# A gated feed-forward and an FP4 feed-forward as one stage, with the FP4 weights quantised between the gated products

## The reference

```
# end of block 5 (XN holds the block's input plus its gated attention, "y")
y2 = y * rsqrt(mean(y*y) + 1e-6) * ff_norm_w
y  = y + (silu(y2 @ ff_w1) * (y2 @ ff_w3)) @ ff_w2        # 256 -> 1024 -> 256
x  = x + y
# block 6, on layernorm(x): a feed-forward whose inputs and weights go through FP4
def fp4_quant_dequant(x):              # blocks of 16 along the last dimension
    scale = max(max|x| / 6, 1e-12);  q = nearest of 0 .5 1 1.5 2 3 4 6, with sign
    return q * scale
gate, up = fq(x) @ fq(w_gate).T, fq(x) @ fq(w_up).T       # 256 -> 704
x = x + fq(silu(gate) * up) @ fq(w_down).T                # 704 -> 256
```

## Time and profile before

| | us |
|---|---|
| median of three executions | 3038.64 (3038.64, 3038.64, 3042.05) |
| the profiled execution | 3042.65 |
| its span | 3040.4 |
| gated stage, from its first instruction to its last | 2810.66 to 2909.45 |
| FP4 stage | 2910.26 to 3035.35 |
| PE busy, of the span | 2752.3 (91%) |
| DVE busy, of the span | 1401.3 (46%) |
| ACT busy, of the span | 1071.5 (35%) |

### The profile page before, as it was taken

One profiled execution on the slowest core, in us unless ns is written; L12 is line 12 of the kernel. 1 busy time (PEld: TensorE's weight loads), 2 busy tenths in 40 slices (PEclk: granted clock), 3 DMA queues, 4 the chain that ended last, 5 costly groups with the idle time before them and its releaser, 6 DMA issues. The chain is left out here.

```text
span 3040.4 us, 95394 instructions
## 1 busy us (share of the span) xinstructions
PE 2752.3 (91%) x43460; PEld 1885.8 (62%) x43460; DVE 1401.3 (46%) x2411; ACT 1071.5 (35%) x1480; POOL 478.3 (16%) x406
## 2 busy tenths in 40 slices
PE   6999999999997699988999999999868998897858
PEld 3666666666665566655666666666547777776445
DVE  3444544535445711135545454544445454444268
ACT  2333333333333321123343434434334454543123
POOL 2424233243332000001000000000001111111000
PEclk9999999999997599999999999999979999999869
DMA  2110111101100000130111111110110000000000
GB/s 84 35 35 24 39 29 29 39 25 35 35 2 12 29 28 28 42 107 26 38 29 35 34 35 34 29 40 24 43 36 3 3 4 3 4 3 5 40 31 14
DMA packets 48630, 88.96 MB, mean 29 GB/s; under 512 B 8496, under 2 KB 43120, under 8 KB 46832
## 3 DMA queue, kind: packets, MB, share of 16 engines
q1 hardware_dynamic: 48240, 82.96, 9.1%
HBM read 81.89 MB, written 1.05 MB: 27 GB/s over the span
## 5 line engine op out<-in xcount | busy, mean ns | idle before, releaser
L525 DVE TENSOR_REDUCE x_mx<-banks 128x2 f32<-128x800 f32 (+1 forms) x512 | 507.3, 993 | 305.3 <-PE banks L640 215.9
L726 PE MATMUL banks<-x_wv,x_cT 128*128 128x256 f32 (+1 forms) x1664 | 466.6, 403 | 24.2 <-DVE x_nmb L530 21.1
L584 PE MATMUL banks<-x_cT,x_wk 128*128 128x400 f32 (+1 forms) x1024 | 362.5, 510 | 18.2 <-DMA x_cT<-in_ctx 18.2
L726 PEld LDWEIGHTS banks<-x_wv,x_cT 128*128 128x128 f32 (+1 forms) x1664 | 279.0, 186 | 145.6 <-issue 76.0
L433 ACT ACTIVATE x_PT<-banks,x_kbs 128x1024 f32<-128x1024 f32 (+1 forms) x208 | 231.8, 1114 | 376.8 <-PE banks L692 376.8
L433 ACT ACTIVATE x_PT<-banks 128x1024 f32<-128x1024 f32 (+1 forms) x208 | 213.0, 1024 | 429.8 <-PE banks L692 358.7
L692 PE MATMUL banks<-x_qbd,x_kT 32*128 32x128 f32 x6656 | 294.4, 273 | 0.0
L584 PEld LDWEIGHTS banks<-x_cT,x_wk 128*128 128x128 f32 x1024 | 192.8, 192 | 163.4 <-issue 27.1
L678 PE MATMUL banks<-x_PT,x_V 128*32 128x64 f32 x13312 | 272.1, 222 | 20.7 <-ACT x_PT L433 20.7
L692 PEld LDWEIGHTS banks<-x_qbd,x_kT 32*128 32x128 f32 x6656 | 253.4, 182 | 0.0
L678 PEld LDWEIGHTS banks<-x_PT,x_V 128*32 128x32 f32 x13312 | 204.9, 109 | 73.7 <-ACT x_PT L433 25.8
(11 more groups left out here) (314 smaller groups left out, 3780.2 us busy)
## 6 DMA issues: line engine op xcount, KB each, us to landing
x_cT<-in_ctx SPq DMA_DIRECT2D x96, 400.0 KB, 3.7
x_cT<-in_ctx SPq DMA_DIRECT2D x32, 401.0 KB, 3.6
e_wu<-in_mo_up SPq DMA_DIRECT2D x9, 512.0 KB, 3.8
e_wd<-in_mo_down SPq DMA_DIRECT2D x9, 512.0 KB, 4.6
x_mrow<-in_mask_row SPq DMA_DIRECT2D x1, 3202.0 KB, 11.3
g_w<-in_db_w SPq DMA_DIRECT2D x3, 1024.0 KB, 7.4
d_wqk<-in_db_qk SPq DMA_DIRECT2D x1, 2048.0 KB, 8.1
f_wgu<-in_fp_gu SPq DMA_DIRECT2D x1, 1536.0 KB, 6.2
```

The costliest lines, as they stand in the source:

```text
L525: dve.reduce_max(mx[:, H0[k]:H0[k] + 3:2, kb], g.PS[:, first:first + 2, 0:KBS[kb]], AXX).then_inc(max_read, 1)
L584: last = pe.matmul(PJ[pb][:, 0:KBS[k]], wk[:, c, gg, :], cT[:, (p + 1) % 2, c, KB0[k]:KB0[k] + KBS[k]], start=c == 0, stop=c == KC - 1)
L726: last = pe.matmul(PJ[pb][0:CHK[c], 0:D], cT[:, p, cc, 128 * c:128 * c + CHK[c]], wv[:, cc, :], start=cc == 0, stop=cc == KC - 1)
```

## The change

`gated_mlp` and `fp4_mlp` become one function, `tail_mlps`, in one block, with the tiles of both (prefix `t_`). The stages before it and the final store are the same. The operations on the weights and on the tiles are the same too; these parts differ:

- SP issues `fw` first, then w1 and w3, then the FP4 weights, then w2. ACT waits for `fw` alone before its copies into `XNT`, and PE for w1 and w3.
- Inside the loop over k, DVE does `scale_blocks` of a piece after the multiplications 3, 4, 6, 8, 10 and 12, and `round_blocks` after 5, 7, 9, 11, 13 and 14.
- PE transposes one weight piece after each of the output tiles 1 to 6.
- The layernorm is done tile by tile in the output loop: DVE adds tile t to X, takes its statistics, and normalises tile t-1. The transposes of XN and their copies, which nothing read, are gone. The x tiles 0 and 1 are quantised within that loop.
- From `up(0)` on, the code is that of before.

```diff
-            for dst, src in ((w1[:, :, :], w["w1"]), (w3[:, :, :], w["w3"]), (w2[:, :, :], w["w2"]), (fw[:, :], w["fw"])):
-                sp.dma_start(dst, src).then_inc(w_in, 16)
+            sp.dma_start(fw[:, :], wg["fw"]).then_inc(fw_in, 16)
+            sp.dma_start(w1[:, :, :], wg["w1"]).then_inc(w13_in, 16)
+            sp.dma_start(w3[:, :, :], wg["w3"]).then_inc(w13_in, 16)
+            sp.dma_start(wgu[:, :, :], wf["gu"]).then_inc(gu_in, 16)
+            sp.dma_start(wdn[:, :, :], wf["down"]).then_inc(dn_in, 16)
+            sp.dma_start(w2[:, :, :], wg["w2"]).then_inc(w2_in, 16)
...
+        SCALES = {3: 0, 4: 1, 6: 2, 8: 3, 10: 4, 12: 5}
+        ROUNDS = {5: 0, 7: 1, 9: 2, 11: 3, 13: 4, 14: 5}
...
# scalar
-            act.wait_ge(w_in, 64)
+            act.wait_ge(fw_in, 16)
...
                 act.activation(s1[:, k % 2, :], g.P[k % 2], ACT.Silu).then_inc(s1_out, 1)
+                if k - 1 in SCALES:
+                    magnitude(SCALES[k - 1] % 2, NBMAX)
+            for t in range(NT):
+                act.wait_ge(lve_done, t + 1)
+                act.activation(lsd[:, t:t + 1], lve[:, t:t + 1], ACT.Sqrt).then_inc(lsd_done, 1)
+                if t in (3, 5):
+                    magnitude(t // 2 - 1, D // QB)
+                if 1 <= t <= PIECES:
+                    weight_copies(t - 1)
+            x_copy(0)
+            silu(0)
+            x_copy(1)
...
# vector
                 dve.tensor_tensor(hT[:, k % FFC, 512 * (k // FFC):512 * (k // FFC) + 512], s1[:, k % 2, :], g.P[2 + k % 2],
                                   ALU.mult).then_inc(h_out, 1)
+                if k in SCALES:
+                    p = SCALES[k]
...
+                    scale_blocks(p % 2, piece(p))
+                if k in ROUNDS:
+                    p = ROUNDS[k]
+                    round_blocks(p % 2, piece(p), w_full)
...
             for t in range(NT):
                 dve.wait_ge(o_full, t + 1)
-                dve.tensor_tensor(g.X[:, t, :], g.X[:, t, :], g.P[4 + t % 4][:, 0:D], ALU.add).then_inc(x_done, 1)
+                dve.tensor_tensor(g.X[:, t, :], g.X[:, t, :], g.P[4 + t % 4][:, 0:D], ALU.add).then_inc(x_mid, 1)
+                dve.wait_ge(x_mid, t + 1)
+                dve.bn_stats(lst[:, t, :], g.X[:, t, :]).then_inc(lbn, 1)
+                dve.wait_ge(lbn, 2 * t + 1)
+                dve.bn_aggr(lmv[:, t, :], lst[:, t, :]).then_inc(lbn, 1)
+                dve.wait_ge(lbn, 2 * t + 2)
+                dve.tensor_scalar(lve[:, t:t + 1], lmv[:, t, 1:2], 1e-5, None, ALU.add).then_inc(lve_done, 1)
+                if t >= 1:
+                    normalise(t - 1)
+                if t in (2, 4):
...
+                    scale_blocks(t // 2 - 1, blocks(g.XN[:, t // 2 - 1, :]))
+                if t == 3:
+                    round_blocks(0, blocks(xq[:, :]), xq_full)
+            normalise(NT - 1)
+            round_blocks(1, blocks(xq[:, :]), xq_full, lambda: dve.wait_ge(tx_full, 1))
...
# tensor, in the loop over the output tiles
                 last.then_inc(o_full, 1)
+                if 1 <= t <= PIECES:
+                    if t == 1:
+                        pe.wait_ge(h_out, NH)
+                    transpose_weights(t - 1)
+            pe.wait_ge(x_mid, 5)
+            transpose_x(0)
+            pe.wait_ge(wt_out, 2 * PIECES)
+            up(0)
+            transpose_x(1)
```

More of the change, by code:

```diff
@@ L2238, in _, with magnitude, weight_copies @@
+            sp.dma_start(w2[:, :, :], wg["w2"]).then_inc(w2_in, 16)
         @block.scalar
         def _(act):
+            magnitudes = 0
+            def magnitude(s, nb):
+                nonlocal magnitudes
+                magnitudes += 1
+                act.wait_ge(v_full, magnitudes)
+                act.activation(sets[s]["m"][:, 0:nb, :], sets[s]["v"][:, 0:nb, :], ACT.Abs, scale=BINADE).then_inc(m_full, 1)
+            def weight_copies(k):
+                for c in (0, 1):
+                    act.wait_ge(wt_full, 2 * k + c + 1)
+                    pt = g.P[2 * (k % 2) + c]
+                    if k < 4:
+                        act.activation(wguT[:, c, 384 * k:384 * k + 384], pt[:, 0:384], ACT.Copy).then_inc(wt_out, 1)
+                    else:
+                        d = k - 4
+                        act.activation(wdT[:, 3 * c:3 * c + 3, 128 * d:128 * d + 128],
+                                       pt[:, 0:384].rearrange("p (f n) -> p f n", f=3), ACT.Copy).then_inc(wt_out, 1)
@@ new lines, in x_copy, with h_copies @@
+            def x_copy(t):
+                act.wait_ge(tx_full, t + 1)
+                act.activation(xqT[:, :, :], g.P[4][:, 0:D].rearrange("p (c n) -> p c n", c=KC), ACT.Copy).then_inc(tx_out, 1)
+            def h_copies(t):
+                for c in (0, 1):
+                    act.wait_ge(th_full, 2 * t + c + 1)
+                    if c == 0 and t >= 1:
+                        act.wait_ge(dn_full, t)
+                    act.activation(hqT[:, 3 * c:3 * c + 3, :], g.P[5 + c][:, 0:384].rearrange("p (f n) -> p f n", f=3),
+                                   ACT.Copy).then_inc(th_out, 1)
@@ L2240, in _, with silu @@
+            def silu(t):
+                for k in (0, 1):
+                    act.wait_ge(up_full, 4 * t + k + 1)
+                    if k == 0 and t >= 1:
+                        act.wait_ge(h_full, 2 * t)
+                    act.activation(sg[:, HALF * k:HALF * k + HALF], g.P[k][:, 0:HALF], ACT.Silu).then_inc(sg_out, 1)
             act.wait_ge(ms_done, 2)
             act.activation(sd[:, :], rs[:, :], ACT.Sqrt).then_inc(sd_done, 1)
-            act.wait_ge(w_in, 64)
+            act.wait_ge(fw_in, 16)
@@ L2247, in _ @@
                                    scale=fw[:, c:c + 1]).then_inc(zt_out, 1)
-            for k in range(2 * FFC):
+            for k in range(NH):
                 act.wait_ge(h1_full, k + 1)
@@ L2254, in _, with done @@
+            x_copy(0)
+            silu(0)
+            x_copy(1)
+            for t in range(NT):
+                magnitude(0, I4 // QB)
+                if t + 2 < NT:
+                    magnitude(1, D // QB)
+                if t + 1 < NT:
+                    silu(t + 1)
+                h_copies(t)
+                if t + 2 < NT:
+                    x_copy(t + 2)
         @block.vector
         def _(dve):
+            steps = rounded = 0
+            def done(ins):
+                nonlocal steps
+                steps += 1
+                ins.then_inc(step, 1)
+                dve.wait_ge(step, steps)
@@ new lines, in round_blocks @@
+            def round_blocks(s, out, full, before_out=None):
+                nonlocal rounded
+                nb, t = out.shape[1], sets[s]
+                v, m = t["v"][:, 0:nb, :], t["m"][:, 0:nb, :]
+                rounded += 1
+                dve.wait_ge(v_full, rounded)
+                dve.wait_ge(m_full, rounded)
+                done(dve.scalar_tensor_tensor(v, m, FLOOR, v, ALU.max, ALU.add))
+                done(dve.scalar_tensor_tensor(v, m, FLOOR, v, ALU.max, ALU.subtract))
+                if before_out:
+                    before_out()
+                dve.scalar_tensor_tensor(out, v, -1.0, wide(t["sc"], nb), ALU.mult, ALU.mult).then_inc(full, 1)
@@ L2270, in _ @@
             dve.tensor_tensor(g.X[:, :, :], g.X[:, :, :], g.XN[:, :, :], ALU.add).then_inc(xy, 1)
-            for k in range(2 * FFC):
+            dve.memset(hq[:, I4:IP], 0.0).then_inc(pad, 1)
+            for k in range(NH):
                 dve.wait_ge(s1_out, k + 1)
@@ L2281, in _ @@
+            add(NT - 1)
         @block.tensor
@@ L2301, in _, with transpose_weights @@
                         last.then_inc(full, 1)
+            def transpose_weights(k):
+                pe.wait_ge(w_full, k + 1)
+                for c in (0, 1):
+                    if k >= 2:
+                        pe.wait_ge(wt_out, 2 * (k - 2) + c + 1)
+                    pt = g.P[2 * (k % 2) + c]
+                    for f in range(3):
+                        if k < 4:
+                            last = pe.transpose(pt[:, 128 * f:128 * f + 128], wgu[:, 3 * k + f, 128 * c:128 * c + 128], g.ident[:, :])
+                        else:
+                            fc = 3 * c + f
+                            last = pe.transpose(pt[:, 128 * f:128 * f + 128],
+                                                wdn[:, k - 4, 128 * fc:128 * fc + 128], g.ident[:, :])
+                    last.then_inc(wt_full, 1)
@@ new lines, in transpose_x, with up @@
+            def transpose_x(t):
+                pe.wait_ge(xq_full, t + 1)
+                if t >= 1:
+                    pe.wait_ge(tx_out, t)
+                for c in range(KC):
+                    last = pe.transpose(g.P[4][:, 128 * c:128 * c + 128], xq[:, 128 * c:128 * c + 128], g.ident[:, :])
+                last.then_inc(tx_full, 1)
+            def up(t):
+                pe.wait_ge(tx_out, t + 1)
+                for k in range(4):
+                    if t >= 1:
+                        if k < 2:
```

(38 more changed lines are left out.)

330 lines of the change are left out of this document (86 added, 244 removed).

## The result

| | before | changed |
|---|---|---|
| median, four executions each | 3040.35 us (3038.64 to 3046.18) | 2995.72 us (2989.01 to 2999.0) |
| ratio, 95% interval | | 0.9847 [0.9823, 0.9871] |
| profiled execution's span | 3040.4 us | 2996.8 us |
| first statistics of the gated feed-forward to the end of the span ("the stage") | 229.7 us (from 2810.69) | 183.8 us (from 2812.97) |

The forecast was 2992.3 in a range of 2986 to 3001, against a median of 3038.64: 46.3 us less. The medians differ by 44.6. The median after lies inside that range, and 0.2 us above the narrower range of 2989 to 2995.5 that went with the forecast alone. The stage alone is 45.9 us shorter. The rest of the span, whose program is unchanged, was 2.3 us longer in this execution; so whole times differ by more than many effects here, and the experiments are read from the stage.

A forecast was written before the change was run, and what follows sets the result against it. Two bounds in sequence: PE with idle DVE, then DVE with idle PE. Start -3.9, transposes +5.0, stretch before up(0) -44.5, its clock -2.9: 46.3 us less, 2992.3 against the median 3038.64; range 2986 to 3001.

The forecast's parts named there:

- Part 1: Start of the gated loop: with fw loaded first, PE starts at 2820.4 instead of 2824.28; gain 3.9 us, bounds 0 to 5.8.
- Part 2: Quantisation in the gated loop: DVE lags at most 1.0 us, hidden by 2.5 us of slack; PE's loop keeps 57 us.
- No reserve: Gated loop, iterations 3 to 14: DVE needs 41.9 of 41.2 us, the argument for DVE holding PE.
- Part 3: Output tiles: six times six weight transposes at 0.82 us add 5.0 us to PE's path; the DVE and ACT work is hidden.
- Part 4: Last output tile to tile loop: up(0) starts 2.02 us after PE's last product and takes 4.90 us instead of 7.79.
- The sum: Up to the second multiplication of h: -3.9, +5.0, -44.5 and -2.9 make 46.3 us less, 2963.48 to 2917.2.
- The row with the pause of 3.05 us: Before's trace near its end: a PE pause of 3.05 us left the clock at 1.00; used to expect up(0) at full clock.
- 1: Rival: DVE holds PE in the gated loop; with DVE steps 20% longer 3.6 us, total 2995.9; chance 0.10.
- 2: Rival: clock differs at the two entries; gated loop at full clock -1.9 us, or up(0) at 1.2 GHz +2.9; chance 0.10.
- 3: Rival: quantisation in the gated loop not hidden because waits interlock; 33.2 us, total 3025.5; chance 0.06, whole or in part.
- 5: Rival: the gated loop's start gains nothing, copies wait for the 2 MB; +3.9 us, total 2996.2; chance 0.06.
- 4: Rival: PE drops to 1.2 GHz in gated products and output tiles; +88 us, total 3080, slower; chance 0.02.

The follow-up runs named there:

- e1: Changed kernel with the old loads (w1, w3, w2, then fw) and ACT waiting for all four before its copies; stage 188.03 us against 183.83.
- e2: Changed kernel with all six weight pieces quantised between the gated loop and DVE's first addition; stage 204.95 us against 183.83.
- e4: Changed kernel with six superfluous DVE passes in iterations 4 to 9 of the gated loop; stage 186.82 us against 183.83.
- e6: Changed kernel with the layernorm over all tiles behind the last output tile, x tiles 0 and 1 quantised after it; stage 197.28 us against 183.83.
- e8: Changed kernel with first FP4 product before last output tile, plus 16 superfluous transposes before last h tile; stage 181.25 us, against 181.01 without these transposes.
- e10: e6 plus 42 superfluous, waited-for DVE passes before x tile 0 is quantised; stage 238.55 us against 197.28.

## Why the prediction was right, step by step

- *Part 1*, 3.9 us: right, 4.2 measured by undoing it (e1), 3.9 between the traces. The loop starts 9.68 us into the stage, against 13.59. ACT's first copy was released by PE.
- *Part 2*, nothing: right, and shown by e2 to e4. The slack of 2.5 us agrees with what e4 leaves over. The lag was sized too large, at most 1.0 us against 0.05: I took the multiplication as 0.72 us of DVE, but where the next instruction waits for nothing it starts 0.61 us after it. A scaling iteration and a rounding iteration ask for 6.7 us of DVE together, with 0.18 idle, not 6.98. "No reserve" was nearly true, in the harmless direction. DVE was busy 39.1 of the 41.2 us from multiplication 3 to the loop's end.
- *Part 3*, 5.0 us: too high. The output tiles with transposes took 31.74 us, without them 27.79: 3.95. I priced six transposes by the length of their row (0.82), which includes the end of the last; in the chain they hold PE for 0.66. Output tiles 1 to 6 are 4.11 us apart, not 4.3.
- *Part 4*, 2.0 us and 4.9: right, 1.97 and 4.97, at full clock. The old layernorm and its place were worth 13.5 us (e6).
- *The sum* to the second h multiplication: 46.3 forecast, 47.6 measured (152.79 to 105.18). Of the 1.3, 1.05 is transposes and 0.2 the gated loop, whose clock rose 3.4 us after its start instead of 3.9. This 0.2 is no effect of the change: from its first product to the first output product the loop took 56.7 to 57.0 us in the three traces of before, and 56.7 to 57.2 in the ten of changed kernels whose DVE had no six passes more. The clock at the loop's entry, for which I had allowed 1.9 us either way, moved it by under 0.6.
- *Behind that point* I had expected no change and it was 1.7 us longer, 1.6 of it the last product. The row with the pause of 3.05 us was right for its own trace, and I made a rule of it: of the mechanisms this is the one that failed. Where I used the rule, at `up(0)` with its pause of 1.76 us, the clock did stay up.
- *How near the total came* is in part luck. In the stage, 1.3 us too little before that point and 1.7 too much behind it cancel, so that 45.9 stands beside 46.3. Against the median, the forecast is 3.4 us low: 1.7 because a fourth execution moved the median of before from 3038.64 to 3040.35, and 1.7 because the medians differ by 44.6.
- *Rivals.* 1 needs DVE steps longer than in the rows; they were not (0.96 us), and e4 shows where it would have begun. Its price was also added up wrongly: the ten steps up to iteration 12 are six scalings and four roundings, 27.3 us and not 27.7, which gives 3.2 us instead of 3.6. 2 did not occur: the first entry moved by no more than the traces of one kernel differ, and the second was at full clock. 3 and 5 did not occur; e2 and e1 show what each would look like. 4: not seen; PE's waits in three iterations of e4 left the clock up, and no run made it wait in every one.

## What to carry to other kernels

When a stage bound by one engine stands before a stage whose start is bound by another, what doesn't depend on the first can be placed into it, here at no cost that the traces show, as long as the lateness stays under the slack between the time a buffer comes free and the time it is wanted; work that slack out from the rows and then dose it to find the edge. Count instructions by their start-to-start distance in the chain, not by their own length: the distance was a fifth shorter for six transposes (0.66 against 0.82 us) and an eighth shorter for a multiplication on DVE (0.61 against 0.69). Effects under 5 us can't be judged by whole times that scatter over 10 us, but a stage measured from its own first instruction repeated within 0.2 us in two traces of the changed kernel and within 0.5 in three of the kernel before.

## What the runs showed of the hardware beyond that

- Behind a pause of 3.05 us a short product of 12 records took 2.83 us, at a granted clock of 1.00, in all three traces of one program. In the eleven traces of the others it took 4.2 to 4.9 us, with the clock at 0.50 for a part of it; in ten of them behind the same pause, in e8 behind one of 1.31. A single trace's reading is no rule.
- A pause of 11.2 us (e6) cost the product behind it 2.6 us, one of 13.7 us (e2) 2.3, one of 52.9 us (e10) 2.2, through the clock. Pauses of 0.3 to 0.6 us in a busy stretch (e4) and one of 1.8 us before `up(0)` cost nothing beyond themselves.
